# Two-layer attention and mixture-of-experts kernel on Trainium2: the last stage scatter-adds straight into the output tensor, padding rows are re-addressed, and 39 tiles are worked instead of 40

## What is computed

```python
x = x + L0_xattn(layernorm(x), ctx, ...)
x = x + L0_ffn(layernorm(x), ...)
x = x + L1_xattn(layernorm(x), ctx, ...)          # the third residual
x = x + L1_ffn(layernorm(x), router_w, w1, w2)    # the output

# L1_ffn: T = 2048 tokens, H = 512, I = 352, E = 8 experts, K = 2 of them per token
logits = xf @ router_w.T
topk_vals, topk_idx = top_k(logits, K)
topk_w = softmax(topk_vals)
x_sorted = xf[order // K]                          # the 4096 (token, expert) pairs, by expert
gate, up = split(ragged_dot(x_sorted, w1.T, counts))
y2 = ragged_dot(silu(gate) * up, w2.T, counts)
y = (y2[inv] * exp_w[:, None]).reshape(T, K, H).sum(axis=1)
```

## Time and profile before

| | us |
|---|---|
| three timed runs: median (lowest to highest) | 3170.26 (3169.36 to 3171.73) |
| the profiled execution: its own time | 3171.96 |
| the profiled execution: span of the trace | 3170.2 |
| busy in the span: PE, DVE, ACT, POOL | 2863.4, 1800.8, 1702.8, 1749.3 |
| `layer1_experts`, first DMA issue to last scatter's issue | 2862.6 to 3144.6 |
| `copy_out`, first DMA issue to the end of the span | 3153.6 to 3170.2 |

### The profile page before, as it was taken

How to read it: one execution, slowest core, us unless ns; L and a number is a source line. 1 busy time by engine, 2 the same in 40 slices (tenths; PEclk the granted TensorE clock), 3 DMA queues, 4 the chain that set the end, 5 groups by cost and what they waited for, 6 DMA issues and landing times. The chain is left out here.

```text
span 3170.2 us, 57410 instructions
## 1 busy us (share of the span) xinstructions
PE 2863.4 (90%) x16353; PEld 1637.4 (52%) x16354; DVE 1800.8 (57%) x5358; ACT 1702.8 (54%) x4566; POOL 1749.3 (55%) x2445
## 2 busy tenths in 40 slices
PE   4599999999999969999999999588898998976996
PEld 2366666666666635555555554234444444433663
DVE  4366666666666555344434445377788887862331
ACT  5578778877887623233323334266666666652331
POOL 6567777777777434455445544455566666631221
PEclk9899999999999979999999999799999999998998
DMA  6711211121112164455445547345554444547444
GB/s 240 242 42 55 77 57 47 54 77 57 47 54 81 41 217 140 135 157 157 132 140 157 157 127 215 76 89 108 107 117 106 115 113 106 117 101 280 86 84 106
DMA packets 467800, 365.79 MB, mean 115 GB/s; under 512 B 295472, under 2 KB 366128, under 8 KB 467632
## 3 DMA queue, kind: packets, MB, share of 16 engines
q1 hardware_dynamic: 404832, 285.13, 31.1%
q0 software_dynamic: 16640, 38.05, 6.1%
q10 hardware_dynamic: 46224, 41.36, 4.4%
HBM read 190.62 MB, written 115.11 MB: 96 GB/s over the span
## 5 line engine op out<-in xcount | busy, mean ns | idle before, releaser
L1415 POOL TENSOR_TENSOR e_st<-e_st,e_ws_tile 128x1024 f32<-128x1024 f32 x64 | 123.8, 1934 | 430.4 <-PE e_y L1171 419.6
L752 ACT ACTIVATE a_nrm<-a_mm,a_sc_t 128x128 f32<-128x128 f32 x768 | 291.5, 476 | 123.6 <-POOL a_sc_t L905 123.5
L603 DVE BATCH_NORM_STATS2 a_st<-a_mm 128x6 f32<-128x128 f32 x768 | 170.7, 285 | 290.3 <-PE a_mm L440 208.0
L439 PE MATMUL a_mm<-a_w_hi,a_xq_hi 128*128 128x512 f16 x768 | 297.0, 387 | 23.7 <-POOL a_xq_lo L887 15.3
L1209 ACT ACTIVATE e_hh<-e_ha 128x512 f16<-128x512 f32 x128 | 76.3, 596 | 419.5 <-PE e_ha L1156 418.0
L440 PE MATMUL a_mm<-a_w_hi,a_xq_lo 128*128 128x512 f16 x768 | 296.8, 386 | 0.0
L1304 DVE SCALAR_TENSOR_TENSOR e_hl<-e_ha,e_hh 128x512 f16<-128x512 f32 x128 | 88.5, 691 | 357.4 <-ACT e_hh L1209 357.1
L904 POOL TENSOR_TENSOR a_sc_t<-a_sc_t,a_mhalf 128x4 f32<-128x4 f32 x192 | 204.1, 1063 | 119.8 <-DVE a_sc_t L610 119.5
L1169 PE MATMUL e_y<-e_w2h,e_hh 128*128 128x512 f16 x640 | 242.6, 379 | 0.0
L1170 PE MATMUL e_y<-e_w2l,e_hh 128*128 128x512 f16 x640 | 242.6, 379 | 0.0
L1171 PE MATMUL e_y<-e_w2h,e_hl 128*128 128x512 f16 x640 | 242.6, 379 | 0.0
(11 more groups left out here) (352 smaller groups left out, 8226.9 us busy)
## 6 DMA issues: line engine op xcount, KB each, us to landing
e_st<-in_w SPq DMA_DIRECT2D x128, 512.0 KB, 4.2
disp<-a_empty SPq DMA_DIRECT2D x16, 2084.0 KB, 8.0
e_st<-in_w1b SPq DMA_DIRECT2D x32, 352.0 KB, 3.1
e_xb<-disp ACTq DMA_DIRECT2D x41, 260.5 KB, 2.7
disp<-a_empty SPq DMA_DIRECT2D x4, 2605.0 KB, 21.6
e_xb<-disp SPq DMA_DIRECT2D x40, 260.5 KB, 4.2
a_cx<-in_ctxT SPq DMA_DIRECT2D x32, 256.0 KB, 3.2
a_stage<-in_wprojT SPq DMA_DIRECT2D x16, 512.0 KB, 4.7
```

What stands on the lines that cost most here:

```text
L439: pe.matmul(out, xq_hi[:, n, c, :], w_hi[:, t, c, :], start=(c == 0), stop=False)
L752: ins = act.activation(nrm[:, n % 2, i * P:(i + 1) * P], src[:, i * P:(i + 1) * P], ACT.Identity, bias=sc_t[:, n % 2, 3, i:i + 1], scale=s ...
```

## The change

- `copy_out` is gone. `x4` is gone: `layer1_attention` stores the third residual in the output tensor, and `layer1_experts` adds its rows to the output tensor. The zeroing store of `x4`'s last 128 rows goes with it (six stores of `empty` are left at L397's place).
- The output tensor has no rows behind the 2048, so a padding row needs a real row, and one that no other row of its tile names. A tile's real rows come first and have ascending token numbers t_p. The m-th token that is not in the tile is m + (number of p with t_p - p <= m). DVE makes the matrix `below[p, m] = (m >= t_p - p)` in float16 for each tile, PE sums its columns with one matmul of one moving column (`ones`) into column 352 of the tile's `u` bank, and DVE makes `row` from it: the token number for a real row, m + count for a padding row, which then adds its zeros there.
- New at the block's start: loads of `upper` and `place` ahead of the weights on SP's queue, a conversion of `upper`, a filling of `ones`, one 128-column matmul and a copy of its result, after which `upper[p, m]` is m.
- PE's `gate_up` waits for `led` (the matrix) too. `row` is written in `gated`, behind `ac`, and no longer in `x_low`.
- `most_tiles` = (4096 + 8 x 127) // 128 = 39 tiles are worked, which is the most that 4096 pairs in eight segments can fill. Before, the fortieth was padding alone.

```diff
-def copy_out(nc, x_dram, out):
...
-        def _(sp):
-            for n in range(2):
-                sp.dma_start(dst[n * rows:(n + 1) * rows, :], x_dram[n * rows:(n + 1) * rows, :]).then_inc(done, 16)
-            sp.wait_ge(done, 64)
...
+        most_tiles = (T * 2 + E * (P - 1)) // P
...
-        UB = [s.ps(f"u{n}", [P, INTER]) for n in range(2)]
+        UB = [s.ps(f"u{n}", [P, DM]) for n in range(2)]
...
-            whole = (TILES - most) // 2
+            whole = (most_tiles - most) // 2
...
             sp.dma_start(ident[:], I["ident"]).then_inc(cin, 16)
+            sp.dma_start(upper[:], I["upper"]).then_inc(cin, 16)
+            sp.dma_start(place[:], I["route_consts"][:, 3 * B * E:3 * B * E + B]).then_inc(cin, 16)
...
-            pe.wait_ge(cin, 16)
+            pe.wait_ge(cin, 48)
+            pe.wait_ge(zero_ok, 3)
+            pe.matmul(YB[0][:, 0:P], ones[:], upper16[:], start=True, stop=True).then_inc(first, 1)
...
                 pe.wait_ge(act_ok, i + 1)
-                for g, out in enumerate((GB[q], UB[q])):
+                pe.wait_ge(led, i + 2)
+                pe.matmul(UB[q][:, INTER:INTER + 1], below[:, q, :], ones[:, 0:1], start=True, stop=True)
+                for g, out in enumerate((GB[q][:], UB[q][:, 0:INTER])):
...
+            dve.wait_ge(cin, 48)
+            dve.tensor_scalar(place[:], place[:], -float(TRASH), 0.5, ALU.add, ALU.mult).then_inc(led, 1)
+            dve.tensor_copy(upper16[:], upper[:]).then_inc(zero_ok, 1)
+            dve.memset(ones[:], 1.0).then_inc(zero_ok, 1)
+            dve.wait_ge(first, 1)
+            dve.wait_ge(led, 1)
+            dve.tensor_copy(upper[:], YB[0][:, 0:P]).then_inc(zero_ok, 1)
+            dve.wait_ge(zero_ok, 4)
             def x_low(i, q):
...
-                dve.tensor_copy(row[:, bass.ds(i, 1)], xb[:, q, DM:DM + 1]).then_inc(r_ok, 1)
+                dve.tensor_tensor(part[:, q, 0:1], xb[:, q, DM:DM + 1], place[:, 0:1], ALU.subtract).then_inc(gap, 1)
+                dve.wait_ge(gap, i + 1)
+                dve.tensor_scalar(below[:, q, :], upper[:], part[:, q, 0:1], None, ALU.is_ge).then_inc(led, 1)
+                dve.tensor_copy(token[:, bass.ds(i, 1)], xb[:, q, DM:DM + 1])
...
                 dve.tensor_reduce(gate[:, q:q + 1], gall[:, q, :], AX_X, ALU.add).then_inc(g_ok, 1)
+                own = token[:, bass.ds(i, 1)]
+                dve.tensor_scalar(part[:, q, 1:2], own, float(T), None, ALU.is_ge).then_inc(split, 1)
+                dve.scalar_tensor_tensor(out=part[:, q, 2:3], in0=own, scalar=float(T), in1=own, op0=ALU.is_lt,
+                                         op1=ALU.mult).then_inc(split, 1)
                 dve.wait_ge(silu, i + 1)
+                dve.wait_ge(split, 3 * i + 2)
+                dve.scalar_tensor_tensor(out=part[:, q, 3:4], in0=UB[q][:, INTER:INTER + 1], scalar=place[:, 0:1],
+                                         in1=part[:, q, 1:2], op0=ALU.add, op1=ALU.mult).then_inc(split, 1)
...
+                dve.wait_ge(split, 3 * i + 3)
+                dve.tensor_tensor(row[:, bass.ds(i, 1)], part[:, q, 2:3], part[:, q, 3:4], ALU.add).then_inc(r_ok, 1)
...
-            with pool.Fori(1, TILES // 2) as n:
+            with pool.Fori(1, most_tiles // 2) as n:
...
-        x2, x4 = dram("x2", (T + CAP, DM)), dram("x4", (T + P, DM))
+        x2, out = dram("x2", (T + CAP, DM)), outs[0]
...
-        layer1_experts(nc, I, disp1, expert_of_tile, row_of_tile, tile_oh, x4, added1, w1_dram, w2_dram)
-        copy_out(nc, x4, outs[0])
+        layer1_experts(nc, I, disp1, expert_of_tile, row_of_tile, tile_oh, out.rearrange("b p d -> (b p) d"), added1, w1_dram, w2_dram)
```

More of the change, by code:

```diff
@@ L2060, in layer1_experts @@
         gate = s.sb("gate", [P, 2], F32)
+        most_tiles = (T * 2 + E * (P - 1)) // P
+        place = s.sb("place", [P, B], F32)
+        token = s.sb("token", [P, TILES], F32)
+        part = s.sb("part", [P, 2, 4], F32)
+        below = s.sb("below", [P, 2, P], F16)
+        ones = s.sb("ones", [P, P], F16)
+        upper = s.sb("upper", [P, P], F32)
+        upper16 = s.sb("upper16", [P, P], F16)
         row = s.sb("row", [P, TILES], U32)
@@ L2070, in layer1_experts @@
         GB = [s.ps(f"g{n}", [P, INTER]) for n in range(2)]
[L2071 removed]
+        UB = [s.ps(f"u{n}", [P, DM]) for n in range(2)]
         YB = [s.ps(f"y{n}", [P, DM]) for n in range(2)]
[L2073 removed]
+        (cin, w_ok, xtr, xhi, xlo, gu, silu, act_ok, atr, ahi, alo, yd, yev, zero_ok, meta, g_ok, r_ok, y_free, gchain, led, split, first, gap) = (
             s.sem(n) for n in ("cin", "w_ok", "xtr", "xhi", "xlo", "gu", "silu", "act_ok", "atr", "ahi", "alo",
[L2075 removed]
+                               "yd", "yev", "zero_ok", "meta", "g_ok", "r_ok", "y_free", "gchain", "led", "split", "first", "gap"))
         w_in = [s.sem(f"w_in{e}") for e in range(E)]
@@ L2080, in pipeline @@
         def pipeline(eng, stages):
-            most = max(lead for lead, _ in stages)
+            most = max(n for n, _ in stages)
             for i in range(-most, 0):
-                for lead, f in stages:
-                    if i + lead >= 0:
-                        f(i + lead, (i + lead) % 2)
-            whole = (TILES - most) // 2
+                for ahead, f in stages:
+                    if i + ahead >= 0:
+                        f(i + ahead, (i + ahead) % 2)
+            whole = (most_tiles - most) // 2
             with eng.Fori(0, whole) as n:
                 for q in range(2):
[L2090 to L2095, removed]
+                    for ahead, f in stages:
+                        f(2 * n + q + ahead, (q + ahead) % 2)
+            for i in range(2 * whole, most_tiles):
+                for ahead, f in stages:
+                    if i + ahead < most_tiles:
+                        f(i + ahead, (i + ahead) % 2)
         def first_two(i):
@@ L2135, in gate_up @@
                         xh, xl = (x[:, q, c, :] for x in xT)
-                        pe.matmul(out[:], xh, wh, start=(c == 0), stop=False)
-                        pe.matmul(out[:], xl, wh, start=False, stop=False)
-                        mm = pe.matmul(out[:], xh, wl, start=False, stop=(c == KT - 1))
+                        pe.matmul(out, xh, wh, start=(c == 0), stop=False)
+                        pe.matmul(out, xl, wh, start=False, stop=False)
+                        mm = pe.matmul(out, xh, wl, start=False, stop=(c == KT - 1))
                 mm.then_inc(gu, 1)
@@ L2255, in _ @@
                 ch.clear()
-            pool.wait_ge(added, 16 * TILES)
+            for i in range(most_tiles // 2 * 2, most_tiles):
+                add_rows(i, i % 2)
+            ch.clear()
+            pool.wait_ge(added, 16 * most_tiles)
 def program(nc, I, outs):
@@ L2278, in program @@
         disp0, disp1 = dram("disp0", (TRASH + 2 * T, RW)), dram("disp1", (PAD + P, RW))
-        layer0_attention(nc, I, tokens(x2), disp0, [disp1], [x2[T + n * P:T + (n + 1) * P, :] for n in range(TPE)] + [x4[T:T + P, :], disp1[PAD:PAD + P, :]], scattered)
+        layer0_attention(nc, I, tokens(x2), disp0, [disp1], [x2[T + n * P:T + (n + 1) * P, :] for n in range(TPE)] + [disp1[PAD:PAD + P, :]], scattered)
         with ExitStack() as held:
```

6 lines of the change are left out of this document (3 added, 3 removed).

## The result

The change took 3170.74 us (median of 6 runs beside the changed kernel's) down to **3153.16** (3150.21 to 3158.18, 6 runs): a ratio of 0.9949, 95% interval 0.9935 to 0.9962. One run of the kernel before took 3468.67 and is left out of the ratio. The forecast was 3145.0 with a range of 3140 to 3153. The direction is right; the time lies 8.2 us over the forecast and 0.2 over the range. The interval is about 4 us to either side: it leaves the forecast out, and cannot tell the time from the range's upper end. The profiled execution took 3152.41 us.

The account below looks back on a forecast made before the run. PE was taken to set the pace at 6.28 us per tile, POOL's scatter chain close behind at 5.98, with a serial tail. Terms -19.8 - 6.3 + 2.3 - 1.5 = -25.3 took the median 3170.26 to 3145.0 us, range 3140 to 3153.

Parts of the forecast that it names:

- Step 4: DVE's new work per tile: hidden beside PE's, with 0.9 us cover for `ac`; cost 0, else 3.9 us per 0.1 over.
- Step 1: End of the program: without the copy block the tail behind the last landing shrinks from 20.8 to 1.0 us, -19.8.
- Step 6: Start of `layer1_experts`: two loads delay the weights, but rows and transposes come earlier; -1.5 us, between +2.0 and -3.5.
- the other sign of 6.45: Steady tile loop: the forecast would be wrong if PE's turn exceeded 6.45 us; 6.31 to 6.39 was expected.
- Step 2: Tile loop: 39 tiles are worked, one PE turn less, -6.3 us.
- Step 3: One-column matmul in `gate_up`: costs an exposed weight load of 0.06 us, 39 times, +2.3 us (0 to +4.3).
- rival C: `gate_up`: the new wait and matmul break PE's stream, a 0.27 us hole per tile, 10.5 for 2.3, 3153 us; chance 0.05.
- Step 5: `gated`: the row number comes later, but POOL needs it only a turn later, after `y_evict`; cost 0.
- Step 7: Stores and scatters go to another tensor of the same shapes, and one covered store fewer ends `layer0_attention`: 0.
- Rival A: Tile loop: DVE's compare and neighbours hold POOL's scatter issue, so POOL sets the pace; up to 3159 us, chance 0.08.
- Rival B: Tile loop: scatter-adds into the output land later, making the kernel slower than before; 3179 us at 6.1 landing, chance 0.03.
- Rival D: End and start: closing takes most of the 4.2 us and the start costs; about 3151 us, chance 0.12.

Follow-up runs that it names:

- e10: Changed kernel without the one-column matmul and with the operation that read its column moved behind `ac`: 3150.29 us, ratio 0.9942, PE turn 6.287 us.
- e6: Kernel before with one more, always met, wait of PE (for `xhi`) in `gate_up`: 3171.17 us, ratio 1.0003, PE turn 6.287 us.
- e13: Kernel before with a met PE wait in `gate_up` and a spare DVE operation between silu and `ac`: 3174.07 us, ratio 0.9998, PE turn 6.311 us.
- e8: The changed kernel once more, unaltered, measured in a later round: 3154.33 us, ratio 0.9950 to the kernel before, PE turn 6.433 us.
- e7: Changed kernel with padding rows reusing the previous tile's row; no one-column matmul, `led` wait or two loads; SP awaits the last landing: 3147.13 us, ratio 0.9931.
- e2: Changed kernel with SP instead of POOL waiting for the last scatter's landing: 3153.59 us, ratio 0.9941, end 7.1 us.
- e9: Changed kernel with the DVE operation that reads the matmul's column moved behind `ac`: 3148.92 us, ratio 0.9936, PE turn 6.312 us.

## Why the prediction was wrong

The large terms held in their mechanism: the tail shrank, one turn is gone, PE sets the pace. Step 4 failed: it followed `ac` to the wrong reader. Steps 1 and 6 were mis-sized, and all three fall the same way. The forecast's own sign of being wrong, a tail of over 3 us behind the last landing, appeared (4.1). The turn stayed under the other sign of 6.45, but over the 6.31 to 6.39 it expected.

- *Step 1, no copy block (-19.8).* **Wrong by 3.1.** The block and its tail are gone, but the closing takes 4.1 us, at my upper bound of 4.2 and not 1.0. I chose the row of a closing alone; that closing was of a block in which POOL had sent nothing. The 4.2 us held POOL's drain of 3.3, and the same POOL work ends the program now.
- *Step 2, 39 tiles.* Right: one turn less.
- *Step 3, the matmul (+2.3).* Measured by itself 39 x 0.025 = 1.0. The spacing of 0.06 was over it, and the load, 96 ns long in the trace, runs under the transposes. "A load takes no longer than that" misread its rows: the loads of that chain last 98 ns each and overlap. The Trainium skill's 107 ns in "TensorE: Matmul & The Clock Gate", section "LDWEIGHTS (loading the stationary operand)", is near that length; taken as a cost per tile it would have been 4 times too much.
- *Step 4, DVE's new work (0).* **The step that failed:** "0.9 us cover" for `ac` measured to `a_transpose`'s first weight load at 3024.08. The transposes do have this cover. `gate_up`, whose preparation PE's stream starts only after the wait for `ac`, has about 0.21 us, and the change used 0.33: 0.22 by `ac` and 0.11 by its own new wait. The rest of DVE's new work does cost nothing, as forecast (e10). By the same step's rule, each 0.1 us over costs 3.9: 39 x 0.138 = 5.4 us, in place of the 2.3 + 0 of steps 3 and 4. The place is rival C's (a hole at `gate_up` each tile), at half its 0.27 us, but its cause is not the new wait and matmul alone; e6, e10 and e13 show that it takes the late `ac` too.
- *Step 5, the row number later.* Right: none of POOL's waits in the block ends with `row`.
- *Step 6, the start (-1.5).* **Wrong by 2.3** by the means of the sixth `y_evict` (+0.8). A single trace does not size it: +1.8 in the first two, -0.8 in e8. Transposes came earlier, as forecast. I had counted the third tile's wait of 2.71 us as gone; 2.20 of it stayed, and one of 3.30 for the second tile was new, while the DMA engines were full.
- *Step 7, stores.* Nothing in the runs speaks against 0.
- Rivals A and B did not occur: the scatter is issued in 1.57 us, though the compare runs beside it in 35 of 39 tiles, and lands in 4.8 (median, as before). Rival D, given 0.12, did: closing takes most of the 4.2, and by the means the start costs. That C's figure of 3153 meets the measured time is luck: its hole is half as large, and D's two terms fill the rest.

Sum: 3145.0 + 3.1 (end) + 3.1 (turn, 5.4 for 2.3) + 2.3 (start) = 3153.5, against 3153.16 measured. So close a match is partly luck. The time itself is known to some 4 us, and between the sixth and the last `y_evict` the longer turn costs only 4.5 us (209.1 in the changed kernel, 204.6 in e7); the other 0.9 are turns of the start, counted twice. In the first two traces alone the block starts 2.5 us earlier, its start costs 1.8, the stretch from the sixth `y_evict` to the last scatter saves 2.2 (4.0 forecast) and the end 16.8 (19.8 forecast): 19.6 in all, where the forecast was 25.3.

## What to carry to other kernels

An engine that is busy all the time still has an instruction stream, and a wait in it holds back everything behind, also what belongs to another tile. When something is put between a producer and such a wait, measure the margin to the first instruction behind it whose own preparation is long, not to the reader of the data. And the price of a closing is read from the block that ends in the same kind of work.

## What was not expected of the hardware

- POOL's drain at the end of a block whose last work was an indirect DMA takes 3.2 to 3.3 us after the transfer has landed in the experts blocks and 2.7 in the attention blocks (34 ns in a block where POOL sent nothing); started earlier it still ends 1.6 us behind the landing (e2). Why the two kinds of block differ is open.
- A matmul of one column with its own 128x128 weight load costs 0.025 us in a busy PE (e9 against e10, the load under a transpose), less than half the 0.06 us at which the 128-column ones follow each other.
- A met wait costs about 0.1 us of PE's stream and nothing of PE's time until the stream's margin is used up (e6, e13).
